# The inverse norm of the queries as VectorE's factor behind the scores, in a hybrid network of two attention stacks

## The reference, cut to what matters

```python
q = l2norm(q) * qs
k = l2norm(k) * ksc
q = q * cos * scale + rotate_half(q) * sin * scale
k = k * cos * inv + rotate_half(k) * sin * inv
...
mask = (it < jb) | (it > jb + w) | (jb == -1)
sim = jnp.einsum('bhwie,bhwje->bhwij', bq, bk2) * QK_SCALE
sim = jnp.where(mask, -jnp.finfo(sim.dtype).max, sim)
attn = jax.nn.softmax(sim, -1)
out = jnp.einsum('bhwij,bhwje->bhwie', attn, bv2)
```

## Time and profile before

| | |
|---|---|
| Median of 3 runs | 3809.59 us |
| Lowest and highest | 3805.08 and 3809.89 us |
| Profiled execution, first to last instruction (span) | 3803.9 us |
| PE busy | 3594.4 us, 94% |
| DVE busy | 3264.6 us, 86% |
| POOL busy | 2752.8 us, 72% |
| ACT busy | 2374.7 us, 62% |

### The profile page before, as it was taken

One profiled execution on the slowest core, in us unless ns is written; L12 is line 12 of the kernel. 1 busy time (PEld: TensorE's weight loads), 2 busy tenths in 40 slices (PEclk: granted clock), 3 DMA queues, 4 the chain that ended last, 5 costly groups with the idle time before them and its releaser, 6 DMA issues. The chain is left out here.

```text
span 3803.9 us, 157044 instructions
## 1 busy us (share of the span) xinstructions
PE 3594.4 (94%) x61680; PEld 2336.5 (61%) x61680; DVE 3264.6 (86%) x11515; ACT 2374.7 (62%) x4331; POOL 2752.8 (72%) x2632
## 2 busy tenths in 40 slices
PE   6799999999999999997699689999999999999998
PEld 4466666666666666662466456666666666666665
DVE  6898888888888889865799798889898888889885
ACT  2567667666766767663422257667676766767665
POOL 1788888878888888852144288888887888888883
PEclk9899999999999999998799699999999999999999
DMA  1232323323322332220000132233233232332222
GB/s 46 77 85 71 81 73 78 87 67 74 85 73 69 85 75 66 66 65 16 0 1 6 29 81 72 74 87 78 71 80 76 71 81 74 83 78 68 66 69 57
DMA packets 170286, 250.95 MB, mean 66 GB/s; under 512 B 36544, under 2 KB 67264, under 8 KB 169408
## 3 DMA queue, kind: packets, MB, share of 16 engines
q1 hardware_dynamic: 169536, 240.72, 25.4%
HBM read 38.21 MB, written 1.05 MB: 10 GB/s over the span
## 5 line engine op out<-in xcount | busy, mean ns | idle before, releaser
L592 PE MATMUL stack_work<-stack_w_qkv,stack_xs 128*128 128x512 f32 x2304 | 1148.0, 604 | 34.4 <-ACT stack_sq L883 17.8
L1244 POOL TENSOR_TENSOR stack_roped<-stack_rot_c,stack_rot_s 128x512 f32<-128x512 f32 x768 | 984.6, 1304 | 148.5 <-DVE stack_rot_s L1052 148.2
L1254 POOL TENSOR_TENSOR stack_roped<-stack_roped,stack_rnorm 128x512 f32<-128x512 f32 x768 | 794.6, 1045 | 188.7 <-DVE stack_rnorm L1084 188.7
L883 ACT ACTIVATE stack_sq<-stack_work 128x512 f32<-128x512 f32 x768 | 443.3, 594 | 485.6 <-DVE stack_rot_s L1052 485.1
L1050 DVE TENSOR_TENSOR stack_rot_c<-stack_work,rot_tables 128x512 f32<-128x512 f32 x768 | 526.8, 686 | 130.4 <-PE stack_work L592 112.9
L592 PEld LDWEIGHTS stack_work<-stack_w_qkv,stack_xs 128*128 128x128 f32 x2304 | 400.5, 191 | 384.4 <-issue 323.9
L1270 POOL TENSOR_TENSOR stack_s_m<-stack_s_m,stack_inv 128x512 f32<-128x512 f32 x384 | 400.8, 1044 | 276.4 <-DVE stack_inv L1113 276.1
L1052 DVE TENSOR_TENSOR stack_rot_s<-stack_work,rot_tables 128x512 f32<-128x512 f32 x768 | 521.6, 679 | 0.0
L1061 DVE TENSOR_REDUCE stack_ssq<-stack_sq 128x8 f32<-128x512 f32 x768 | 496.7, 667 | 6.0 <-issue 4.4
L641 PEld LDWEIGHTS stack_bank_o<-stack_p_t,stack_v_w 64*64 64x64 f32 x24576 | 394.5, 135 | 171.9 <-issue 147.4
L600 PE MATMUL stack_work<-ident,stack_roped 128*128 128x128 f32 x3072 | 452.2, 280 | 8.3 <-issue 5.8
(11 more groups left out here) (257 smaller groups left out, 5269.0 us busy)
## 6 DMA issues: line engine op xcount, KB each, us to landing
stack_v_w<-stack_v_nat SPq DMA_DIRECT2D x1152, 128.0 KB
stack_v_w<-stack_v_nat SPq DMA_DIRECT2D x768, 64.0 KB
stack_w_qkv<-table_ffn_qkv SPq DMA_DIRECT2D x192, 96.0 KB, 2.3
stack_w_o<-table_ffn_wo SPq DMA_DIRECT2D x12, 512.0 KB, 4.2
stack_w<-table_ffn_w SPq DMA_DIRECT2D x12, 384.0 KB, 3.3
stack_w<-table_ffn_w SPq DMA_DIRECT2D x12, 192.0 KB, 3.1
x_outer<-L_attn_a_X SPq DMA_DIRECT2D x4, 256.0 KB, 6.9
ret_xpos<-table_xpos SPq DMA_DIRECT2D x1, 1024.0 KB, 6.2
```

What stands on the lines that cost most here:

```text
L592: pe.matmul(bank[:, :], xs[:, T, :], w_qkv[:, g.half, col:col + 512], start=True, stop=True).then_inc(done["proj_" + c], 1)
L883: act.activation(sq[:, i % 2, :], work[(BANK["p_" + c][T] + g.row) % 4][:, :], ACT.Square).then_inc(done["squared_" + c], 1)
L1244: pool.tensor_tensor(roped[:, i, T % 2, :], rot_c[:, i % 2, :], rot_s[:, i % 2, :], ALU.add).then_inc(done["roped_" + c], 1)
L1254: pool.tensor_tensor(r, r, rnorm[:, T % 2, i, :].unsqueeze(2).broadcast_to([P, 8, HD]), ALU.mult).then_inc(done["united_" + c], 1)
```

## The change

The two products by the inverse norm of the queries, `unit` for q0 and q1, are taken out of POOL's slot. PE's transposes of q0 and q1 wait for the ropes instead of the products. `mask_max` takes the column of `rnorm` that belongs to its head as the factor that was 1.0, and waits for "unit_set" of its tile. The keys are multiplied as before.

```diff
@@ turn @@
-                wait(pe, "united_" + c, t)
+                wait(pe, ("roped_" if c[0] == "q" else "united_") + c, t)
@@ mask_max @@
+                wait(dve, "unit_set", t)
                 wait(dve, "scored", t)
+                apart(dve, t)
                 wait(dve, f"pe_pt{j}", t - 2)
                 apart(dve, t)
                 first = 0 if T > 0 else 2 * WINDOW
                 for hp in range(PAIRS):
+                    i, h = CHUNKS.index(f"q{hp // 4}"), 2 * (hp % 4) + j
                     last = dve.tensor_tensor_reduce(s_m[:, T % 2, j, hp, :], bank_s[j][:, 64 * hp:64 * hp + 64],
-                                                    mask[:, first:first + 2 * WINDOW], 1.0, LOWEST, ALU.add, ALU.max,
-                                                    smax[:, T % 2, j, hp:hp + 1])
+                                                    mask[:, first:first + 2 * WINDOW], rnorm[:, T % 2, i, h:h + 1],
+                                                    LOWEST, ALU.add, ALU.max, smax[:, T % 2, j, hp:hp + 1])
@@ slot of gpsimd @@
                 rope(*at(1), "k0")
                 rope(*at(1), "q0")
-                unit(*at(2), "q0")
                 unit(*at(2), "k0")
                 scale_probs(*at(4), 1)
-                unit(*at(2), "q1")
                 scale_probs(*at(4), 0)
```

## The result

The changed kernel takes 3847.24 us in the median of four runs (3845.71 to 3848.51), the kernel before 3807.34 on the same chip (3804.12 to 3809.89). The ratio is 1.0106, with a 95% interval from 1.0092 to 1.0120: slower by 1%, or 39.9 us. The profiled execution has a span of 3843.0, against 3803.9.

The account below looks back on a forecast made before the run. PE was taken as the bound, busy 496.95 of 500 us, with DVE's work free only until PE waits for it; 48 × (0.65 + 0.13) = 37 us on the median 3809.6 gave 3847 us, range 3804 to 3868.

Parts of the forecast that it names:

- The products are worth 0: On POOL, dropping the products for q0 and q1 frees 401 us of busy time but shortens the run by 0 us.
- A column costs 60 ns, 1.0 us per tile: On DVE, each of 16 masks per tile takes 60 to 63 ns more by reading a column: 1.0 us per tile.
- Place one: Clamp L1073 falls behind POOL's k1 product and is held, so PE's L626 waits for hidden product L1141: +0.65 us per group.
- Place two: In the chain to the gelu, L1077's shrinking hold absorbs most of the masks' delay, leaving +0.13 us per group.
- Sum, 37 us: Over the whole run, 48 groups times (0.65 + 0.13) us, added to the median of 3809.6: 3847 us.
- the column hidden: Rival at DVE's masks: the column is hidden or costs under 53 ns, giving 3805 to 3815 us; chance 25%.
- Both places in full: Rival: the clamp's place and the gelu chain lose 0.65 + 1.0 us per group, 79 us, giving 3889; chance 9%.
- It gets faster: Rival: POOL, with 2.1 us less per tile, holds DVE less and the gelu wait goes, giving 3788 us; chance 6%.
- POOL holds the masks themselves: Rival: masks wait for POOL's instructions, one hold per tile giving about 3889, one per mask 3000 us in all; chance 2%.

Follow-up runs that it names:

- 12 and 14 columns: The kernel before with 12 or 14 of a tile's 16 masks reading a column of ones instead of constant 1.0: 3803.18 and 3849.09 us.
- Undoing it alone: The changed kernel with the hidden product L1144 moved ahead of the clamp L1073 in slots with T = 1: 3813.71 us, ratio 1.0019.
- the two edits at the holds of the clamp and of L1077: Each on the kernel before: the clamp as tensor_reduce, 3769.28 us; POOL's product for k1 right behind k0's, 3771.85 us.

## Why the prediction was right

It said 3847 us, and 3847.24 was measured. That the two agree so closely is luck: the forecast started from 3809.6, which is 2.3 us above the 3807.34 measured beside the changed kernel, and its sum of 37.4 was 2.5 below the measured 39.9. The mechanism is what was right, step by step.

- *The products are worth 0*: shown, 3806.46 without them. POOL's idle time in front of the scaling went from 276.1 us to 641.8 in the changed kernel, 366 of the 380 us that it was relieved of. The prediction had 401 us, and 2352 busy, where 2372.3 was measured: where POOL's instructions follow one another, each begins some 0.05 us before the last one's end (1073.34 against 1073.39), and the prediction had counted this overlap, some 20 us in 384 products, as busy time.
- *A column costs 60 ns, 1.0 us per tile*: shown. One block of 16 lasts from 1081.79 to 1085.01, 3.22 us in place of 2.27, so 59 ns a mask; the mean of the custom instruction rose by 58 (217 to 275). The first mask's start is this row:

```profile
1081.79 0.23 DVE L1098 CUSTOM_DVE_ANT_0 stack_s_m<-stack_bank_s,band,stack_rnorm 128x64 f32<-128x64 f32 x1
```

- *Place one, +0.65 us*: shown by its rows, with 0.59 us of PE's idle time in the steady groups, 0.68 in the mean of 44, and by the step between 12 and 14 columns. Undoing it alone gave 0.70 by the medians and 0.66 by the distance between groups. The prediction called this line of waits new; it was there with 4 instances before, and has 44 now, not 48.
- *Place two, +0.13 us*: 0.12 us by the rows (0.96 less 0.84), and 0.16 by the medians or 0.14 by the distance between groups in the kernel in which only this place is left.
- *Sum, 37 us*: 39.9. The distance from one group to the next in the steady part gives the same: in the kernel before L676's wait ends at 985.70 and, three groups on, at 1183.16, which is 65.82 us a group; in the changed one L626's ends at 955.06 and 1154.91, 66.62. That is 0.80 a group, 0.78 by the forecast.

```profile
985.70 1.12 PE L676 MATMUL stack_work<-stack_x_c,stack_w 128*128 128x512 f32 x2 [0.45 <-ACT stack_hid L983]
...
1183.16 1.12 PE L676 MATMUL stack_work<-stack_x_c,stack_w 128*128 128x512 f32 x2 [0.45 <-ACT stack_hid L983]
```

```profile
955.06 0.66 PE L626 MATMUL stack_work<-ident,stack_s_m 128*128 128x128 f32 x4 [0.59 <-DVE stack_hid L1144]
...
1154.91 0.66 PE L626 MATMUL stack_work<-ident,stack_s_m 128*128 128x128 f32 x4 [0.59 <-DVE stack_hid L1144]
```

Three more signs came out otherwise than the prediction had them. DVE's busy time rose by 112 us and not by 190: the masks added 185, but L1077's held time counts as busy too, and it fell from 137.5 us to 55.7 in all, while the product L1135, of which more below, rose by 11.5. I had seen that shrinkage at place two and hadn't carried it to the total. The wait at L676 was to be 0.6 us and is 0.5 (24.0 us in 46 instances); the groups are 0.14 us further apart by place two all the same, and where the missing part of it lies wasn't found. And one POOL instruction did get longer: 46 subtractions, one per group, last 1.50 us now instead of 1.05. The longest of each kind, before and after:

```profile
L1262 POOL TENSOR_TENSOR stack_s_m<-stack_s_m,stack_smax x384: 1032/1044/1068, 139.6 to 3756.5; 128x512 f32<-128x512 f32 x192
L1244 POOL TENSOR_TENSOR stack_roped<-stack_rot_c,stack_rot_s x768: 1259/1278/1741, 109.5 to 3729.1; 128x512 f32<-128x512 f32 x192
```

```profile
L1265 POOL TENSOR_TENSOR stack_s_m<-stack_s_m,stack_smax x384: 1032/1046/1507, 139.3 to 3793.9; 128x512 f32<-128x512 f32 x192
L1247 POOL TENSOR_TENSOR stack_roped<-stack_rot_c,stack_rot_s x768: 1260/1277/1292, 109.2 to 3763.0; 128x512 f32<-128x512 f32 x192
```

In the kernel before, the ropes had such a maximum (1741 ns) and the subtractions none. The collision with a long DVE instruction has moved from one to the other, by some 21 us of busy time each. The timeline of the changed kernel has the DVE instruction, and POOL's beside it:

```profile
1034.73 0.98 DVE L1135 TENSOR_TENSOR stack_x_c<-stack_x_c,stack_std 128x512 f32<-128x512 f32 x1
```

```profile
1035.12 1.50 POOL L1265 TENSOR_TENSOR stack_s_m<-stack_s_m,stack_smax 128x512 f32<-128x512 f32 x1
```

It is the product L1135 (L1132 before), which reads two tiles from SBUF. Here it is POOL that is held, since DVE's instruction had started first, and L1135 in turn lasts 990 ns in the median in place of 724. Nothing suggests that this costs time: with 12 columns L1135's counterpart lasts even 1.23 us, and the time is that of the kernel before.

Of the rivals, *the column hidden* was wrong on its price, but 12 columns of 16 show how near it was. *Both places in full* was wrong since L1077's hold had 0.88 us to give. *It gets faster* was wrong for this change, but its figure of 3788 was too modest for what lay there: either of the two edits at the holds of the clamp and of L1077 is worth 34 to 37 us in the kernel before. *POOL holds the masks themselves* was wrong: the 3072 mask instructions with the column last 225 to 291 ns, and none is held for a POOL instruction.

## What to carry to other kernels

In this kernel an instruction of DVE is held until POOL's running one is over. Work added ahead of it cost nothing as long as it still started before POOL's next instruction (0.72 us per tile), and beyond that (0.84 us per tile) it brought a new hold of up to 1.09 us, of which PE's slack of 0.39 us took off a part. So the quantity to read from the rows isn't the idle time in total, but the distance from the held instruction's start to the next start on the other engine, and what PE needs behind it. And busy time may be waiting: the clamp's 940 ns for 32 elements was the lead that paid, 1% of the time when it was followed, while 400 us of real work on POOL were worth nothing. And where PE is busy 499.9 of 500 us, the distance between groups still shows costs that neither its busy time nor its waits do.

## What the runs showed that I had not expected

- How sharp the step is: a clamp that starts 0.13 us ahead of POOL's product is let through, one that starts 0.01 us ahead is held for 1.09 us. 12 and 14 columns differ by 46 us.
- A clamp written as `tensor_reduce` takes 0.22 us beside a working POOL, the `tensor_scalar` form 0.94 to 1.09, for the same 32 results.
- Two quite different edits, each a few lines, took away the same 34 to 37 us, and together no more: with either, PE has no row of waits left in the middle of the tile loop.
